# A fused FFN, attention, FFN kernel: row maxima of the attention taken four steps earlier, and the work between the steps laid out anew

## What is computed

```
q, k, v = x @ W_q.T, x @ W_k.T, x @ W_v.T        # 16 heads of 8
q, k    = rope(q), rope(k)
scores  = q k^T / sqrt(8)                        # 256 x 256 per batch and head
out     = softmax(scores) @ v @ W_o.T
x       = x + out
```

## Time and profile before

| | |
|---|---|
| median of 3 runs | 401.68 us (401.1 to 401.76) |
| the profiled execution | 405.68 us |
| its span in the profile | 403.9 us |
| granted TensorE clock, mean over the span | 0.924 |
| PE, matmuls | 313.2 us busy (78%) |
| DVE | 230.8 us busy (57%) |
| ACT | 199.1 us busy (49%) |
| POOL | 162.7 us busy (40%) |

### The profile page before, as it was taken

How to read it: one execution, slowest core, us unless ns; L and a number is a source line. 1 busy time by engine, 2 the same in 40 slices (tenths; PEclk the granted TensorE clock), 3 DMA queues, 4 the chain that set the end, 5 groups by cost and what they waited for, 6 DMA issues and landing times.

```text
span 403.9 us, 6408 instructions
## 1 busy us (share of the span) xinstructions
PE 313.2 (78%) x2104; PEld 176.7 (44%) x2104; DVE 230.8 (57%) x573; ACT 199.1 (49%) x451; POOL 162.7 (40%) x295
## 2 busy tenths in 40 slices
PE   1759749999246798989898989888874896699960
PEld 0125436666113444544454544444441363466640
DVE  8945312433176777878878787787834621243422
ACT  2108113544225568686868777876652531055520
POOL 3924730665347434342424332431221176035660
PEclk9999997999756699999999999999999798699995
DMA  7960134101210000000000000000000011501017
GB/s 219 169 270 20 54 105 79 42 39 41 96 40 1 2 1 2 2 0 2 2 1 2 2 0 2 3 1 2 2 0 2 0 52 52 153 20 47 39 41 214
DMA packets 24271, 18.37 MB, mean 45 GB/s; under 512 B 4944, under 2 KB 22608, under 8 KB 23984
## 3 DMA queue, kind: packets, MB, share of 16 engines
q1 hardware_dynamic: 21744, 12.84, 12.5%
q0 software_dynamic: 2496, 5.13, 3.5%
HBM read 10.26 MB, written 7.71 MB: 44 GB/s over the span
## 4 chain that ended last, share of the span: by engine, by line
DVE 30%; PE 27%; POOL 15%; issue 13%; another core or an unknown queue 7%; DMA 4%; ACT 2%; SPq 1%; POOLq 0%; DVEq 0%; ACTq 0%
PE bank L822 21%; DVE negmax L715 11%; POOL y_by_token L342 9%; DVE xn L579 5%; PE bank L974 3%; DVE sh L637 2%; DMA xs<-y_by_token 2%; DVE qT L708 2%; DVE rs L731 2%; DVE stats L589 1%; DMA y_by_token<-ys,xg 1%; POOL parts L374 1%; POOL parts L371 1%; POOL parts L373 1%
## 5 line engine op out<-in xcount | busy, mean ns | idle before, releaser
L715 DVE TENSOR_REDUCE negmax<-bank 128x2 f32<-128x512 f32 x128 | 82.1, 684 | 14.0 <-PE bank L822 13.6
L511 ACT ACTIVATE probs<-bank 128x512 f32<-128x512 f32 x128 | 72.1, 607 | 25.9 <-PE bank L822 25.4
L342 POOL DMA_INDIRECT y_by_token<-ys,xg x46 | 44.6, 970 | 57.6 <-DVE ys L683 30.0
L822 PE MATMUL bank<-kT,qT 128*128 128x512 bf16 x128 | 50.2, 393 | 10.6 <-DVE negmax L715 5.3
L822 PE MATMUL bank<-qT,kT 128*128 128x256 bf16 x256 | 48.9, 273 | 5.5 <-DVE qT L708 3.9
L822 PE MATMUL bank<-rgu,xgT 128*128 x92 | 48.8, 614 | 0.5 <-ACT xgT L481 0.5
L680 DVE TENSOR_TENSOR rh<-rsg,bank 128x256 f32<-128x256 f32 x46 | 19.4, 421 | 46.6 <-ACT rsg L489 46.6
L333 POOL DMA_INDIRECT xs_sorted<-xs,slot x32 | 31.5, 984 | 34.6 <-ACT xs L471 13.8
L519 ACT COPY kT<-bank 64x1024 bf16<-64x1024 bf16 x32 | 32.2, 1006 | 19.8 <-PE bank L974 19.6
L822 PE MATMUL bank<-probs,vx 128*32 128x256 f32 x512 | 39.0, 389 | 0.1
L489 ACT ACTIVATE rsg<-bank 128x256 f32<-128x256 f32 x46 | 17.6, 383 | 38.4 <-PE bank L822 38.4
(11 more groups left out here) (105 smaller groups left out, 488.8 us busy)
## 6 DMA issues: line engine op xcount, KB each, us to landing
xg<-xs_sorted SPq DMA_DIRECT2D x10, 258.0 KB, 4.7
rgu<-in_rgu SPq DMA_DIRECT2D x1, 2048.0 KB, 19.8
xs<-y_by_token SPq DMA_DIRECT2D x8, 256.0 KB, 3.5
xs_sorted<-xg SPq DMA_DIRECT2D x1, 1483.5 KB, 16.3
x<-in_x SPq DMA_DIRECT2D x4, 256.0 KB, 3.3
rdn<-in_rdn SPq DMA_DIRECT2D x1, 1024.0 KB, 16.3
out_x<-x SPq DMA_DIRECT2D x4, 256.0 KB, 2.6
y_by_token<-ys,xg POOLq DMA_INDIRECT x46
```

The source lines that it names most:

```text
L342: g.indirect_dma_start(y_dram, bass.IndirectOffsetOnAxis(ap=xg[:, j, D:ROW].bitcast(U32), axis=0), ys[:, j, :], None, bounds_check=N + SLO ...
L511: a.activation(probs[:, h % 8, :], stbank[st_bank(u, h)][:], ACT.Exp, scale=float(DH) ** -0.5).then_inc(exp_done, 1)
L715: v_.tensor_reduce(negmax[:, w, t, h0 + 2 * pair:h0 + 2 * pair + 2], sbank[k % 2][:].rearrange("p (a s) -> p a s", a=2), AX.X, ALU.max, ne ...
L822: return t_.matmul(o_, l, r, start=start, stop=stop, **k)
```

## The change

Same arithmetic and the same instructions, in another order and with other banks:

- `Turn.unit(n)` puts `scores` and `maxima` four steps earlier: steps 0 to 3 of turn i do the last four of batch i, steps 4 to 11 the first eight of batch i+1, steps 12 to 15 the next four of batch i+1. Turn -1 therefore has 12 of them, turn 7 only four.
- The two halves become one run of 16 steps n. Transposes, copies, projections and ropes stand at steps of their own on PE, DVE and ACT; `values` is issued as one block of 16 matmuls instead of two of 8, and that of the last four heads moves to step 3 of the next turn.
- The projections `qkv0`, `qkv1` leave the score banks and join the two work banks, which now serve 12 uses.
- POOL's order in a turn is another, and the `Fori` with its helper waits is gone; all turns are written out.

```diff
-        uses = ["back", "qa", "ka", "mb", "oT", "wo", "xT", "qb", "kb", "ma"]
+        uses = ["qkv0", "qkv1", "qa", "ka", "back", "mb", "oT", "qb", "kb", "wo", "xT", "ma"]
...
+            def unit(self, n):
+                k = n + H - HH + AHEAD
+                b, half, k = (self.i + k // H, k % H // HH, k % HH)
+                return (b, half, k) if 0 <= b < B else None
...
+        def attention(turn):
+            for i in range(-3, B + 1):
+                turn(Turn(i))
```

ACT:

```diff
+                for n in range(H):
+                    if T.e:
+                        exponentials(n)
+                    if n in (2, 3) and T.m:
+                        copy_keys(0, n - 2)
+                    if n == 4 and T.f:
+                        act.wait_ge(pv_done, 4 * i)
+                        a.copy(pvs[:].rearrange("p f s -> p (f s)"), pvbank[:]).then_inc(pv_copied, 1)
+                    if n in (7, 8) and T.pr:
+                        first(n - 7)
+                    if n == 9 and T.f:
+                        act.wait_ge(filled["oT"], i)
+                        a.copy(oT[:], work[uses.index("oT") % 2][:, 0:L]).then_inc(emptied["oT"], 1)
+                    if n in (10, 11) and T.m:
+                        copy_keys(1, n - 10)
+                    if n in (12, 13) and T.pr:
+                        second(n - 12)
+                    if n == 14 and T.nx:
+                        act.wait_ge(filled["xT"], i + 4)
...
```

DVE:

```diff
+                for n in range(H):
+                    if T.unit(n):
+                        maxima(*T.unit(n))
+                    if n in (0, 1) and T.pr:
+                        rope(n)
+                    if n == 2 and T.m:
+                        copy_queries("qa")
+                    if n == 5 and T.f:
+                        divide()
+                    if n == 6 and T.e:
+                        copy_queries("mb")
...
+                    if n == 8 and T.nx:
...
+                    if n == 10 and T.m:
+                        copy_queries("qb")
+                    if n == 12 and T.f:
...
+                    if n == 14 and T.m:
+                        copy_queries("ma")
+                    if n == 15 and T.nx2:
+                        moments_of(4, u)
```

PE (`scores` waits, as before, for the maximum two steps back, and at the first step of a half for the copies of that half's queries and keys):

```diff
+                for n in range(H):
...
+                    if T.e:
+                        scores_t(n)
+                    if T.unit(n):
+                        scores(*T.unit(n))
+                    if n == 0 and T.pr:
+                        project(0)
+                        project(1)
+                    if n == 1 and T.m:
+                        pe.wait_ge(part3, 2 * (i + 1) + 2)
+                        turn_parts("qa")
+                        turn_parts("ka")
+                    if n == 3 and T.f:
+                        values(i - 1, 3)
+                    if n == 5 and T.f:
+                        w = work_bank("back")
+                        pe.wait_ge(pv_copied, i)
...
+                    if n == 6 and T.e:
+                        pe.wait_ge(m_split, 2 * i + 2)
+                        turn_parts("mb")
+                    if n == 7 and T.e:
+                        values(i, 0)
+                    if n == 8 and T.f:
+                        w = work_bank("oT")
+                        pe.wait_ge(emptied["back"], i)
...
+                    if n == 9 and T.m:
+                        turn_parts("qb")
+                        turn_parts("kb")
+                    if n == 10 and T.e:
+                        values(i, 1)
+                    if n == 11 and T.f:
+                        w = work_bank("wo")
+                        pe.wait_ge(emptied["oT"], i)
...
+                    if n == 12 and T.nx:
+                        w = work_bank("xT")
+                        pe.wait_ge(a_xn, 2 * (i + 3) + 2)
...
+                    if n == 13 and T.e:
+                        values(i, 2)
+                    if n == 14 and T.m:
+                        pe.wait_ge(m_split, 2 * (i + 1) + 1)
+                        turn_parts("ma")
```

More of the change, by code:

```diff
@@ L197, in link @@
                 self.n += 1
[L198 to L214, removed]
+                self.eng.wait_ge(self.s, self.n)
@@ L224, in early @@
             def early(self, late):
[L226 to L260, removed]
+                c = self.i - late - (B - CHUNKS + 1)
@@ L437, in turn @@
                     ffn_rstd(1, T.early(0))
-            attention(pool, turn, st, 2 * (1 + 6))
+            attention(turn)
             ffn_rstd(1, CHUNKS - 1)
@@ L537, in turn @@
                 second = lambda t: part(t, 2, rem, (slice(1, 6, 4), slice(4, 6)), rem_ready, part2)
[L538 to L562, removed]
@@ new lines, in turn @@
+                for n in range(H):
[17 more added lines that the diff above has]
+                        act.wait_ge(filled["xT"], i + 4)
+                        a.copy(xnT2[:, v, :], work[uses.index("xT") % 2][:, 0:L]).then_inc(emptied["xT"], 1)
+                    if i == B and n in EARLY_TURNED:
+                        copy_chunk(1, EARLY_TURNED.index(n))
+                        if n >= HH:
+                            a.activation(table_use[:, 2:3], neghalf[:, 0:1], ACT.Tanh)
@@ L568, in _ @@
             a.activation(table_use[:, 1:2], neghalf[:, 0:1], ACT.Exp)
-            attention(act, turn)
+            attention(turn)
             ffn(1)
@@ L754, in moments_of @@
                     ins.then_inc(a_stats, 1)
-                if not T.looped and i == -3:
+                if i == -3:
                     moments_of(3, v)
@@ L812, in _ @@
             ffn(0)
-            attention(dve, turn, st, 2 * 2)
+            attention(turn)
             ffn(1)
@@ L1080, in turn @@
                         project(0)
                         project(1)
+                    if n == 1 and T.m:
[7 more added lines that the diff above has]
+                        pe.wait_ge(pv_copied, i)
+                        for c in range(4):
+                            ins = t_.transpose(w[:, c * P:(c + 1) * P], pvs[:, c % 2, (c // 2) * P:(c // 2 + 1) * P], ident)
+                        ins.then_inc(filled["back"], 1)
@@ new lines, in turn @@
+                    if n == 9 and T.m:
[6 more added lines that the diff above has]
+                        pe.wait_ge(emptied["oT"], i)
+                        for t in range(2):
+                            ins = mm(w[:, t * P:(t + 1) * P], oT[:, t * P:(t + 1) * P], wo[:])
+                        ins.then_inc(filled["wo"], 1)
@@ L1088, in _ @@
                 pe.wait_ge(s_, SLOT_TILES)
-            attention(pe, turn)
+            attention(turn)
             ffn(1)
```

253 lines of the change are left out of this document (95 added, 158 removed).

## The result

The changed kernel takes 412.33 us (406.32 to 413.16, 4 executions) against 401.50 before (401.1 to 401.76): a ratio of 1.023, 95% interval 1.014 to 1.033. The forecast was 410.7 in a range of 401 to 416, slower with a chance of 0.78. It was slower. Two later comparisons of the same two kernels gave 1.034 (1.028 to 1.040) and 1.034 (1.030 to 1.039).

A forecast was written before the change was run, and what follows sets the result against it. No engine is full; in-order chains bound the turns. Prologue +2.0, turn 0 +0.2, turns 1 to 4 +6.0, turn 5 +1.9, turn 6 -0.6, turn 7 -0.5 sum to +9.0 on 401.7: 410.7 us, range 401 to 416.

The forecast's parts named there:

- What bounds it: Attention turns: no engine full; a chain through POOL's split, run twice a turn, leaves DVE idle 2.85 us.
- What the change takes away: Around the split: four more maxima cover its 1.30 us, so a turn would lose up to 2.85 us.
- the loop was worth nothing: `Fori` around the turns: costs zero, since the turns at its begin and end are no longer than their neighbours.
- What it adds: Steady turns: four new waits (`ka`, `back`, `kb`, step 12) make a turn 23.0 us against 21.49, +1.5.
- The marks of the layout by hand: Times within one turn, added up from trace latencies: `ka` 4.38 us through step 12 at 19.0, turn closing at 23.0.
- The open term: ACT: an exponential behind a key copy, not in the trace, 0.91 or 1.01 us; 1.01 taken, worth 0.2 a turn.
- the announced signs: Profile after: turns 22.5 to 23.5 us, PE 1 to 1.5 before transposes once a turn, first `scores_t` 1 to 3 later.
- `back` behind two key copies: ACT in a steady turn: `back` waits for `pvs`, which stands behind both key copies, and starts at 9.44 us.
- the draw rival: Whole kernel: one wait hidden (`oT` 1.0 us a turn, key copies ahead of `pvs` 1.5), 396 to 405 us; chance 0.18.
- The prologue: Turn -1: `ka` behind rope 1 and twelve steps instead of eight bring the first `scores_t` 2.0 us later.
- Its other moves cost nothing: POOL's reordered work in a turn: never late, with over 1 us of cover, so zero cost.
- The rival of a lower clock: Steady turns: PE's idle gaps lower its clock, about 7 us more per half-clock turn, 418 us and up; chance 0.08.

The follow-up runs named there:

- the best version: changed kernel with `ka`, `oT`, `pvs`, `back` and division moved, three steps of lead, rstd ahead of rotations, moments at step 13; 0.988 and 0.994 of the kernel before.
- the run with `pvs` alone: changed kernel with only ACT's copy of the value bank (`pvs`) moved ahead of the second key copy; 1.034 of the kernel before, turns 23.25 us.
- The run with `pvs` and `back`: changed kernel with `pvs` ahead of the second key copy, `back` and division at step 4, three steps of lead; 413.54 us, 1.028 of the kernel before.

## Why the prediction was right

**What bounds it.** Right: no engine's work but a chain of in-order waits. DVE's busy time in a turn is 16.8 us after and 17.25 before, while the turn grew, and moving single instructions shortened it.

**What the change takes away.** The 2.85 us of DVE idle time around the split are gone, and the waits view of 139 to 300 us has no wait of PE on POOL. That the loop was worth nothing rests on the kernel before, whose turns inside and outside it both take 21.49; no run takes it away alone. What the lead is worth by itself was not shown either: in the changed layout four steps instead of two save 0.36 us a turn, and the best version, at 20.14 against 21.49, has a lead of three and the new order together.

**What it adds.** The marks of the layout by hand, beside turn 2: `ka` 4.38, measured 181.79 - 177.50 = 4.29; `back` 9.44, measured 9.42; step 8 12.35, measured 12.30; `kb` 14.99, measured 14.95; step 12 19.0, measured 19.09; the turn 23.0, measured 23.05. The marks hold because most durations and hand-over latencies stayed those of the rows before; some of the closeness is luck. The open term, the time from a key copy to the exponential behind it, came at 0.89 (183.16 to 184.05) and 1.04 (184.67 to 185.71), where 1.01 was put; the exponential between the two copies took 0.62 and not 0.49; and single misses of up to 0.13 us cancelled until `back`. The recorded terms themselves add to 12.33 at step 8 and the last ones to 21.62, slips of 0.02. One of the announced signs was off: PE stood 0.53 us before `qa` and 0.82 before `ka`, not 1 to 1.5.

**Weak in its reading.** "`back` behind two key copies" named one of two waits on this link; `scores` of step 4, mentioned in passing, held as much, as the run with `pvs` alone showed. In the same way the draw rival's prices for a hidden link (1.0 for `oT`, 1.5 for `pvs`) were right for the first, 1.1, and wrong for the second: alone it made the turn 0.2 longer, and 1.1 shorter only with two more edits. And "about 0.2% from no change" was too fine: the intervals of these comparisons reach 0.3 to 0.9% to either side.

**The prologue was mis-sized**: +2.0 was put, +3.6 measured (+2.8 in the shortest of three traces; the sign said 1 to 3). The step left out is POOL's rstd, which the change put behind the rotations. "Its other moves cost nothing" holds in the steady turns, where POOL has time to spare, and not in turn -2, where DVE's layer norm waits 1.62 us for it. Of this 0.6 to 1.4 us reached the first `scores_t`; with rstd moved back the prologue is 2.2 us longer than before the change, close to the +2.0.

**The clock.** The rival of a lower clock did not come true where it was placed: the steady turns were granted 1.00 throughout in spite of four waits near 1 us. It did in turn 0 of two of the three traces. This is the windows view of 4 us each from the start of turn 0 in the third trace of the changed kernel:

```profile
140.18:144.18 4.00, 2.94 (x18) 1.72 (x18) 3.97 (x15) 1.19 (x2) 0.73 (x1) 1.00 0.00 0
144.18:148.18 4.00, 1.65 (x15) 1.15 (x16) 2.12 (x5) 2.81 (x4) 2.16 (x6) 1.00 0.00 0
148.18:152.18 4.00, 3.72 (x22) 2.27 (x26) 2.62 (x4) 2.20 (x5) 1.40 (x7) 0.57 0.00 0
```

PE was busy 1.65 of 4 us, with one wait of 2.28 us for the keys in it, and in the next 4 us it was granted 0.57 on average, for the most part the lower level, 1.2 GHz. This turn took 22.3 us, and the second trace has the same dip and 22.4 us. In the first trace PE was busy 1.71 us in the same 4 us, yet was granted 1.00 behind it, and the turn took 21.06. So 1.3 us of the change's cost come and go. By the Trainium skill (TensorE: Matmul & The Clock Gate, section on the clock gate) the gate follows how busy the array has been; the two dips agree in direction, and the first trace shows that the same stand-still can also pass without one.

## What to carry to other kernels

When work is spread over the steps of a software pipeline, ask of each piece not only when its input is there but what stands behind it in the same queue: a transpose that waits 1 us for a bank holds up the scores of every step after it. Walk the steady turn once with durations and latencies from the trace, from a wait back round to itself; here that gave the turn to 0.05 us before the kernel ran (part of it luck), and then which single instruction to move. Where two waits end together, removing one gains nothing.

## What the runs showed that was not expected

The same kernel, the best version, took 106.2 us behind the attention in one profiled execution and 99.4 in another. The windows views of the second FFN (columns as in the earlier trace rows) show the granted clock of PE, here in the trace of its last run:

```profile
303.00:313.00 10.00, 8.32 (x33) 3.24 (x32) 5.91 (x23) 4.48 (x11) 0.43 (x1) 0.72 0.00 0
...
333.00:343.00 10.00, 6.66 (x32) 3.87 (x31) 3.32 (x6) 1.71 (x7) 0.00 (x0) 1.00 0.59 161
```

and here in that of the run before:

```profile
303.40:313.40 10.00, 8.65 (x29) 3.80 (x30) 5.14 (x19) 3.54 (x8) 0.00 (x0) 0.50 0.00 0
...
333.40:343.40 10.00, 5.15 (x19) 4.30 (x20) 2.72 (x5) 1.08 (x2) 0.72 (x1) 0.54 0.61 165
```

These stretches were granted 0.72 and 1.00 in one execution and 0.50 and 0.54 in the other. But the clock is the smaller part of the 6.7 us. PE's timelines show where they arise: its first transpose for an expert tile (`tab,xg`) starts 46.4 us behind the last `back` in the one and 53.3 in the other, and from there on the two executions nearly keep step. The links ahead of it are DVE's additions of the shared expert's output to `x` (`x<-bank`, L610), which free the bank for PE's next block (`shdn,sh`). In the first trace of the changed kernel DVE starts each 2.1 to 2.8 us after its work before, as soon as PE has filled the bank. In the slower execution of the best version one of them starts at 335.35, after DVE has stood for 12.9 us, though PE's block (322.53 to 324.58) had been done for 10.8; behind it PE stands 10.2 and ACT 13.3 us. The other execution has two smaller ones, of 6.1 and 6.5 us. Until this point the slower one, with its lower clock, was 2.7 us behind. The run with `pvs` and `back` (106.8 us) has such a stand-still of DVE, too, of 12.8 us, the first trace of the changed kernel (100.1 us) none.

The first FFN has the like: before the change DVE stood 5.7 and 7.2 us there, in the first trace of the changed kernel at most 2.8, and the first `tab,xg` came at 63.2 against 54.6 us, which is all of the 8.5 us. What DVE waits for the trace does not name. The low clock of 0.54 comes with and behind PE's wait, and may be its effect as well as a cause of more time.

Such a difference is more than most of the edits here are worth, so they had to be judged by the turns and not by the total. The medians of the kernel before moved too, 401.5, 398.5, 403.9 and 402.9 us in the four comparisons (the second was taken on another chip than the last two). What holds DVE there stays open, and so does what decides the clock.
